# Six buffer slots in place of four for the signs of the ternary weights

## The reference

```python
def ternary_quant(w_fp32, g=64):
    w = w_fp32.astype(jnp.bfloat16)
    w_g = w.reshape(-1, g)
    scale = jnp.clip(jnp.mean(jnp.abs(w_g), axis=-1, keepdims=True), 1e-08, None)
    q = jnp.clip(jnp.round(w_g / scale), -1, 1)
    ...
gate, up = jnp.split(jnp.einsum('bsd,hd->bsh', x, wq_gu), 2, axis=-1)
h = jax.nn.silu(gate) * up
return jnp.einsum('bsh,dh->bsd', rms_norm(h), wq_p)
```

## Time and profile before

| | |
|---|---|
| median of three runs | 3192.96 us (3188.8 to 3195.98) |
| the profiled execution | 3194.99 us, of which its span is 3193.2 us |
| PE busy | 3018.1 us, 95% of the span |
| VectorE (DVE) busy | 1927.4 us, 60% |
| ScalarE (ACT) busy | 1686.5 us, 53% |
| GpSimd (POOL) busy | 748.3 us, 23% |

### The profile page before, as it was taken

The page is one execution under the profiler, slowest core; times in us unless marked ns, Lnnn a source line. Parts: engine busy times, 40 slices in busy tenths (PEclk is TensorE's granted clock), DMA queues, the critical chain, the costliest instruction groups (busy, mean ns, idle before and its releaser), DMA issues. The chain is left out here.

```text
span 3193.2 us, 52651 instructions
## 1 busy us (share of the span) xinstructions
PE 3018.1 (95%) x16214; PEld 1150.0 (36%) x16214; DVE 1927.4 (60%) x2349; ACT 1686.5 (53%) x3156; POOL 748.3 (23%) x644
## 2 busy tenths in 40 slices
PE   6789999999998999999999999999988899999999
PEld 3434444444564122222222222222233344444444
DVE  6763222221676999999999999999913322222221
ACT  5543333333111588888888888888830233333332
POOL 0044444444443000000000000000012344444444
PEclk9999999999998799999999999999999999999999
DMA  3221100111333011111111111111237111111000
GB/s 121 73 88 40 40 17 25 38 40 41 101 104 85 18 30 30 29 29 29 29 30 29 29 30 28 28 29 29 77 123 244 53 40 40 40 39 39 23 23 33
DMA packets 163964, 161.01 MB, mean 50 GB/s; under 512 B 62552, under 2 KB 100824, under 8 KB 163808
## 3 DMA queue, kind: packets, MB, share of 16 engines
q1 hardware_dynamic: 163808, 159.30, 16.8%
HBM read 111.48 MB, written 47.19 MB: 50 GB/s over the span
## 5 line engine op out<-in xcount | busy, mean ns | idle before, releaser
L1742 DVE TENSOR_REDUCE at_neg_max<-at_max_ps 128x1 f32<-128x1024 f32 x1024 | 1207.4, 1220 | 43.3 <-PE at_max_ps L1628 24.8
L1730 ACT ACTIVATE at_probs<-at_score_ps 128x512 f32<-128x512 f32 x2048 | 1057.7, 604 | 187.3 <-PE at_score_ps L1648 179.5
L1628 PE MATMUL at_max_ps<-at_km,at_q 48*128 48x512 f16 x2048 | 708.0, 395 | 13.8 <-PEq L1221 8.1
L1648 PE MATMUL at_score_ps<-at_q,at_ks 50*128 50x512 f16 x2048 | 628.0, 386 | 56.6 <-ACT at_probs L1730 40.8
L1655 PE MATMUL at_out_ps<-at_probs,at_v 128*32 128x512 f32 x4096 | 551.1, 610 | 0.1
L1648 PEld LDWEIGHTS at_score_ps<-at_q,at_ks 50*128 50x128 f16 x2048 | 153.6, 94 | 670.0 <-ACT at_probs L1730 555.0
L977 DVE SCALAR_TENSOR_TENSOR f_h<-f_up_ps,hr_factor,f_gate 128x512 f32<-128x512 f32 x128 | 96.1, 751 | 477.6 <-ACT f_gate L1051 475.5
L1924 POOL TENSOR_TENSOR rows<-rows,bias 128x512 f32<-128x512 f32 x32 | 39.4, 1265 | 1425.0 <-ACTq L1863 1337.8
L407 DVE SCALAR_TENSOR_TENSOR f_h<-f_up_ps,hr_factor,f_gate 128x512 f32<-128x512 f32 x112 | 83.9, 749 | 394.2 <-PE f_up_ps L746 240.7
L1051 ACT ACTIVATE f_gate<-f_gate_ps 128x512 f32<-128x512 f32 x128 | 76.4, 597 | 353.8 <-PE f_up_ps L1124 353.8
L1073 POOL TENSOR_TENSOR f_h_lo<-f_h,f_h_hi 128x512 f16<-128x512 f32 x128 | 148.2, 1158 | 379.4 <-ACT f_h_hi L1040 379.4
(11 more groups left out here) (145 smaller groups left out, 3642.4 us busy)
## 6 DMA issues: line engine op xcount, KB each, us to landing
rows<-x SPq DMA_DIRECT2D x40, 1024.0 KB, 5.7
x<-rows SPq DMA_DIRECT2D x16, 1024.0 KB, 4.4
f_raw<-units SPq DMA_DIRECT2D x48, 256.0 KB, 2.6
at_q<-qk_parts SPq DMA_DIRECT2D x384, 32.0 KB, 1.7
rows<-x SPq DMA_DIRECT2D x32, 256.0 KB, 2.9
at_q<-at_max_parts SPq DMA_DIRECT2D x512, 1.0 KB
att<-at_out SPq DMA_DIRECT2D x256, 32.0 KB
ao_a<-att SPq DMA_DIRECT2D x8, 1024.0 KB
```

What stands on the lines that cost most here:

```text
L1628: done = nc.tensor.matmul(max_ps[u % 2][:, half * QB:(half + 1) * QB], q[k][rows, j // SLOTS, h * QB + c * P:h * QB + (c + 1) * P], km[k][ ...
L1648: nc.tensor.matmul(score_ps[pos % RING][:], ks[k][rows, kc * P:(kc + 1) * P], q[k][rows, j // SLOTS, h * QB:(h + 1) * QB], start=True, sto ...
L1730: nc.scalar.activation(probs[:, kc % PBUF, j, :], score_ps[pos % RING][:], ACT.Exp, scale=HD ** -0.5).then_inc(exps, 1)
L1742: nc.vector.tensor_reduce(neg_max[:, h, column:column + 1], max_ps[u % 2][:], AX.X, ALU.max, negate=True).then_inc(maxed, 1)
```

## The change

One constant is changed. The buffer `sgn` grows by half, from 4 to 6 slots of 1 KB in each partition, the slot of unit u is u % 6, and ScalarE's sign of unit u waits for the finished weights of unit u-6 in place of u-4. Everything else stays.

```diff
--- before.py
+++ after.py
@@ -144,7 +144,7 @@
 UG = 2 * HC
 RAW = 4
 MW = 3
-SW = 4
+SW = 6
```

## The result

The changed kernel takes 3173.56 us, the median of six runs (3170.86 to 3177.55), against 3194.47 (six runs, 3188.8 to 3200.72) before: a ratio of 0.9938, 95% interval 0.9923 to 0.9952, so it is faster by 0.5 to 0.8%. The forecast was 3174.

What follows compares the result with a forecast made beforehand. The loop of ScalarE's sign waiting for VectorE's weights, and PE for the sign, was taken as the bound; six terms sum to 19.2 us, giving 3173.8 from the median 3192.96, forecast 3174, range 3166 to 3184.

Steps and rivals of the forecast that it cites:

- The turn: First 200 us: sign, scale, difference, weights form a loop; four slots make a pair 6.97 us, six remove the wait.
- start, to the sum at 42.92: Stage start: PE's hold by the sign at 27.91, 0.62 us, perhaps a second like it, goes; 0.9 us gained.
- 16 units, to 98.97: From 42.92: a pair falls to 5.87 us, bound by PE with its Silu wait; 9.1 us gained.
- 5 units, to 117.55: From 98.97: tile 1 chunks on PE and ScalarE's cast ahead of the Silu; 17.75 against 18.58 us, 0.8 gained.
- 6 units, to 138.05: From 117.55: units mostly without norms, one with two small products; 17.6 against 20.50 us, 2.9 gained.
- to 146.84: From 138.05: VectorE's unit, factor arithmetic, scaled copy and square, to the difference; 7.2 against 8.79 us, 1.6 gained.
- last window, to 191.20: From 146.84: VectorE bounds; ScalarE runs ahead, so idle time in front of the difference goes; 3.9 us gained.
- Rival 1: Last window gives nothing: VectorE meets POOL's sums at the worst point or PE's clock drops; 3178 to 3181, chance 0.15.
- The seam: Behind 191.34: PE's products or chains from them set the pace, loads shift along, so all comes 19 us earlier.
- Rivals 3 and 4: Late rows, loads or POOL sums absorb the stage's gain, or another guard holds the sign; 3193, chance 0.08 together.
- 5: Rival: PE's granted clock falls from 2.4 to 1.2 GHz; slower, 3226 if all 30 products are hit; chance 0.04.
- Rival 2: All PE waits behind the sign come back, as the Silu wait overlaps more than thought; 3168, chance 0.08.

Runs made afterwards that it cites:

- late only: Changed kernel with six slots, but up to unit 37 the sign waits for the weights of u-4 as before; one execution, 3194.11 us.
- the two one-sided openings: Changed kernel with the four-slot guard kept from unit 38 on, or only up to unit 37; one execution each, 3177.94 and 3194.11 us.

## Why the prediction was right, point by point

**The turn and what opens it.** Right. Sign, scale, difference and weights were a closed turn of 3.18 and 3.79 us; the wait of 57.9 us is gone. Five slots open it as well, which the prediction had no need to say but could have: weights(u-5) come from VectorE's unit u-2, and that is early enough.

**The new bound.** Right: PE's unit and the Silu behind the scale. Forecast 2.57 + 3.30 = 5.87 us a pair, measured 2.52 + 3.29 = 5.81; forecast wait for the Silu 0.7 us, measured 0.60. The Silu moved ahead of the scale shows that it was this wait and not one that hides another.

**The sum.**

| term | forecast | measured |
|---|---|---|
| start, to the sum at 42.92 | 0.9 | 0.5 |
| 16 units, to 98.97 | 9.1 | 9.55 |
| 5 units, to 117.55 | 0.8 | 0.94 |
| 6 units, to 138.05 | 2.9 | 2.92 |
| to 146.84 | 1.6 | 1.59 |
| last window, to 191.20 | 3.9 | 3.98 |
| sum | 19.2 | 19.5 |

The start has the right size by luck. The gate product behind the table's load came 2.1 us earlier (38.61 to 36.49), and the clock, which fell behind the gap, took 1.6 us back. The prediction saw the load as neutral. One pair of profiles can't settle this term: the sum of unit 9 stands anywhere from 40.83 to 43.02 in the six profiles of five to seven slots whose order is the same up to there, and at 42.92 and 42.12 in the two whose guard is that of four slots (before, and late only). Behind unit 9 the size is firm: from its sum to the sum of squares it is 167.4 us before and 148.4, 148.3, 148.5 and 148.4 in both profiles of the changed kernel, with five and with seven slots. That is 19.0 us where the terms behind the start add up to 18.3; the 16 units gave the most of the difference, since the pair takes 5.81 us and not 5.87.

**The last window.** Right as a size and as a mechanism: the idle time ahead of the difference went (5.0 us in the earlier trace rows, 0.4 in the changed kernel) and nothing took its place; the two one-sided openings give 4.3 and 4.6 us for it against 4.0 in the changed kernel. Rival 1 did not come. What it feared is there, though: POOL's operations are longer, 21.81 us for the same 12 against 16.93. By the Trainium skill ("SBUF — State Buffer", section "SBUF: two separate sides") one side holds the shared ports for an instruction and the other blocks. The trace agrees in kind, and shows that both sides lose. Of the changed kernel, a sum on POOL and three of VectorE's operations beside it:

```profile
142.79 3.36 POOL L665 TENSOR_TENSOR f_sqsum<-f_sqsum,f_sq 128x512 f32<-128x512 f32 x1 [2.27 <-ACT f_sq L593]
```
```profile
143.00 0.68 DVE L431 SCALAR_TENSOR_TENSOR f_diff<-f_scl,f_mag 128x512 bf16<-128x512 bf16 x1
...
144.94 1.75 DVE L397 SCALAR_TENSOR_TENSOR f_h_lo<-f_whole,hr_factor,f_h_hi 128x512 f16<-128x512 f32 x1
146.62 1.75 DVE L431 SCALAR_TENSOR_TENSOR f_diff<-f_scl,f_mag 128x512 bf16<-128x512 bf16 x1
```

POOL's operation starts at 142.79, but VectorE goes on at its usual 0.68 us and is held only at 144.94, for 1.75 us in place of 0.74: so, by these rows, POOL stood for about 1.8 us first (3.36 less 1.56), and then VectorE. The difference at 146.62 meets POOL's next sum. VectorE's loss a collision is still near 1.0 to 1.1 us, and it is now the difference at times, which had not been held in the last window before.

**The seam.** Right: everything behind 191.34 moved by 19.5 us, the wait for the residual included. Rivals 3 and 4 did not come, nor did 5: the granted clock is 1.00 from 42.38 to 131.30, and no matmul of 128x512 in it takes over 0.45 us. Rival 2, all waits given back, would have needed the Silu's wait to stay at the 0.26 us of before; it grew to 0.60.

**The total.** The stage gives 19.5, the medians of the runs 20.9 apart. The difference lies inside the spread: the single runs of one kernel lie 7 to 12 us apart here. That the forecast of 3174 meets 3173.56 so closely is therefore in part luck: it started from a median of 3192.96, and from the 3194.47 of the six runs its sum of 19.2 would have given 3175.3. The other six runs of the changed kernel give 3173.72 against 3193.28, 19.6 apart.

## What to carry to other kernels

When the guard of a ring of slots is a count of some other engine's results, write down in whose step that result is made and what that step itself waits for; if it leads back to the waiting instruction, the slots are not a buffer but part of a cycle, and one more slot than closes it gives the whole gain, while further ones give nothing. The size of the gain is then the walk of the next engine in its own order, read at places where the trace already shows it unheld. And an instruction that stands in an in-order queue ahead of a wait costs in the closed cycle and is free in the open one: the same move of the Silu cost 5 us with four slots and gained 12 with six, so such moves are to be tried again after the cycle is open; the two together take the kernel from 3193 to about 3160 us.

## What the runs showed of the hardware that was not expected

- The same gap on PE did not always do the same to its clock. At the table's load, six of eight profiles with a gap of 1.68 to 2.02 us were followed within 0.9 us by three to four us at the lower level, two were not, and none of five with at most 1.19 us was. At the end of the stretch a gap of 2.85 us was followed by the lower level in one profile (late only) and not in four (both of the changed kernel, five and seven slots). The falls cost 1.6 and 1.7 us.
- The granted clock of a window can miss this: in the changed kernel it reads 1.00 from 28.0 to 30.5 us, where six matmuls of 128x512 last 0.58 to 0.63 us and not 0.38. The two records disagree there.
- With VectorE busy without a pause, two of POOL's twelve 128 x 512 sums took 3.36 and 3.57 us in place of 1.56, while each of VectorE's operations that met one stayed at 1.4 to 1.8 us.
- The first Silu brings a table with which the magnitudes, signs, copies and squares run as well: with the Silu first there is one load, at 0.75 us, and the one in unit 7 is gone. A load took 1.28 us.
